# Layer 1's output product for two tiles at once, transposed, in three rounded terms

## The reference

```python
h = layernorm(x) * (1 + scale) + shift
Q, K, V = relu(h @ Wq + bq), relu(h @ Wk + bk), h @ Wv + bv        # 16 heads of 64
# causal linear attention with cos and sin weights of the position (scan over t):
num = qc @ S_cos + qs @ S_sin;  den = max(qc . z_cos + qs . z_sin, 1e-6)
out = (num / den).reshape(B, T, 1024)
x = x + gate * (out @ Wo + bo)                                     # Wo: 1024 x 128
# then a router over 16 experts and the layer's mixture of experts on layernorm(x)
```

## Time and profile before

| what | value |
|---|---|
| median of three runs | 860.9 us (857.6 to 861.99) |
| profiled execution, its span | 860.6 us |
| instructions | 32362 |
| loop of layer 1, PE full | about 310 to 763 us |

### The profile page before, as it was taken

How to read it: one execution, slowest core, us unless ns; L and a number is a source line. 1 busy time by engine, 2 the same in 40 slices (tenths; PEclk the granted TensorE clock), 3 DMA queues, 4 the chain that set the end, 5 groups by cost and what they waited for, 6 DMA issues and landing times.

```text
span 860.6 us, 32362 instructions
## 1 busy us (share of the span) xinstructions
PE 798.8 (93%) x13678; PEld 695.9 (81%) x13678; DVE 611.5 (71%) x1776; ACT 434.6 (50%) x944; POOL 394.6 (46%) x399
## 2 busy tenths in 40 slices
PE   6999984489998799999999999999999999999998
PEld 5777764489997678888889888889888888878887
DVE  7897785357773676676677776787877778757865
ACT  6555533244542665656546566566574645523322
POOL 4357685604544473554645754556643533500000
PEclk9999996599998999999999999999999999999999
DMA  9824000163421200000010000100000000038661
GB/s 294 259 67 161 27 29 13 41 184 102 135 86 45 83 27 4 3 28 4 15 40 4 28 4 3 53 4 4 4 3 3 5 3 3 4 79 148 143 126 39
DMA packets 67904, 49.65 MB, mean 58 GB/s; under 512 B 5322, under 2 KB 62778, under 8 KB 67377
## 3 DMA queue, kind: packets, MB, share of 16 engines
q1 hardware_dynamic: 64288, 42.41, 18.4%
q0 software_dynamic: 3328, 5.16, 1.8%
q10 hardware_dynamic: 144, 0.02, 0.0%
HBM read 33.20 MB, written 16.10 MB: 57 GB/s over the span
## 4 chain that ended last, share of the span: by engine, by line
PE 72%; issue 13%; DVE 6%; DMA 3%; ACT 2%; another core or an unknown queue 1%; SPq 1%; POOL 1%; PEldq 0%; PEld 0%; DVEq 0%; ACTq 0%; POOLq 0%
PE psum L1560 11%; PE psum L1665 7%; PE psum L1716 6%; PE psum L1690 6%; PE psum L1244 6%; PE psum L2349 5%; PE psum L1595 5%; PE psum L1627 5%; PE psum L2367 4%; PE psum L1705 4%; PE psum L1607 3%; PE psum L1578 3%; PE psum L1279 3%; DMA sb_e_x<-disp 1%
## 5 line engine op out<-in xcount | busy, mean ns | idle before, releaser
L1560 PE MATMUL psum<-sb_wkv,sb_a_hs 128*128 128x512 f32 x384 | 122.1, 426 | 1.3 <-ACT sb_a_hs L2036 0.7
L2248 POOL TENSOR_TENSOR sb_a_qr<-sb_h,sb_a_csq 128x512 f32<-128x512 f32 x64 | 81.0, 1288 | 92.0 <-PE psum L1690 88.1
L2248 POOL TENSOR_TENSOR sb_a_qr<-sb_a_qp,sb_a_csq 128x512 f32<-128x512 f32 (+1 forms) x64 | 72.2, 1149 | 94.6 <-PE psum L1690 94.6
L1844 ACT ACTIVATE sb_a_vr<-sb_a_va,sb_consts 128x520 f32<-128x520 f32 x128 | 86.6, 726 | 14.6 <-DVE sb_a_va L2106 14.3
L310 POOL DMA_INDIRECT disp<-sb_h,sb_slot x64 | 67.9, 1062 | 32.2 <-issue 16.9
L1560 PEld LDWEIGHTS psum<-sb_wkv,sb_a_hs 128*128 128x128 f32 x384 | 63.6, 190 | 13.5 <-issue 1.2
L1183 POOL DMA_INDIRECT chosen<-sb_m_h3t,sb_e_row x40 | 39.4, 984 | 69.3 <-ACTq L1357 49.2
L1665 PE MATMUL psum<-sb_a_mid,sb_a_qr 64*64 64x65 f32 x2048 | 70.9, 218 | 0.0
L1244 PE MATMUL psum<-sb_e_xt,sb_e_ws 128*128 128x320 f32 x384 | 65.5, 327 | 5.4 <-issue 4.3
L1690 PE MATMUL psum<-sb_a_vr,sb_a_kb 64*64 64x130 f32 x1920 | 70.1, 272 | 0.0
L1244 PEld LDWEIGHTS psum<-sb_e_xt,sb_e_ws 128*128 128x128 f32 x384 | 59.6, 198 | 9.2 <-issue 5.2
(11 more groups left out here) (289 smaller groups left out, 1986.2 us busy)
## 6 DMA issues: line engine op xcount, KB each, us to landing
sb_h<-turned SPq DMA_DIRECT2D x32, 256.0 KB, 5.5
sb_e_w<-in_w SPq DMA_DIRECT2D x24, 256.0 KB
chosen<-sb_empty SPq DMA_DIRECT2D x8, 512.0 KB, 6.1
sb_a_g<-chosen SPq DMA_DIRECT2D x12, 256.0 KB, 3.1
disp<-sb_empty SPq DMA_DIRECT2D x4, 650.0 KB, 9.9
sb_e_x<-disp SPq DMA_DIRECT2D x7, 325.0 KB
sb_a_wo<-in_wo SPq DMA_DIRECT2D x4, 512.0 KB, 4.5
out<-sb_x SPq DMA_DIRECT2D x7, 256.0 KB, 3.9
```

The source lines that it names most:

```text
L1560: ins = pe.matmul(self.values_bank(i) if kv else self.bank[0], hs[:, part, at:at + P], self.Wkv[ws][:, h, w], start=(k == 0), stop=(k == 2))
L1844: ins = act.activation(self.Vr[i % 2][:, :, k, :], self.Va[i % 3][:], ACT.Copy, scale=self.c[("cos1", "sin1")[k]][:, n:n + 1])
L2248: ins = g.tensor_tensor(self.Qr[i % 2][:, k, :, t], qp, rows(self.csQ[:, k, c * P + t.start:(c + 1) * P], PH), ALU.mult)
```

## The change

- The product is done for two tiles (pair p) at once, at steps i = 4p + 5, and transposed: Wo is stationary, the turned outputs of two tiles are moving, 256 columns wide. Three rounded terms, eight blocks each: 24 matmuls. The exchange of halves is done in the moving operand's reading order.
- ACT's three copies become two: one of bank 3 into a plain buffer oTf (`outputs_scalar`) and, behind it, one that rounds it into oT1[0] (`outputs_high`). POOL makes the rest oT1[1] by a subtraction (`outputs_low`), in every step, behind the queries and ahead of everything else of its step; ACT's next first copy waits for it.
- The gate is no longer in the weights: ACT copies the transposed product to y with the gate's column as scale (`output_gated1`), between its two copies; PE turns y back in the next step (`output_returned`, i = 4p + 6), and DVE adds two tiles to x at once. POOL's four `gate_out` and four loads of Wo go away; Wo is loaded once early (`raw_o`, 512 KB) and split by ACT and DVE at expert 5 of layer 0 (two more pieces; experts 1 to 4 have two each already).
- In the loop the statistics for the router begin at step 3 instead of 2, POOL's roots for it at step 4 instead of 3. `tiles_normed` and `tiles_turned` stay where they are.
- Behind the loop the last pair's product comes after `gate_up_tensor(1, 2)`; the last tiles' statistics, turn and logits, and group 6's router weights (`weights1_parts`) come later.
- To make room some buffers move into others' space, and the DMA scratch of the program is set to 8 KB.

```diff
@@ -1463,7 +1468,7 @@
-        self.Wog = [sb(f"a_wo{k}", [P, HD // P, D]) for k in range(2)]
+        self.Wo = [sb(f"a_wo{k}", [P, HD // P, D], F32R) for k in range(2)]
@@ -1498,9 +1504,8 @@
-        halves = sb("a_ot", [P, HD // P, P])
-        spare = self.h3T[:, (NT - G4) * P:].rearrange("p (m t) -> p m t", t=P)
-        self.oT1 = [[halves[:, 0:PH, :], spare], [halves[:, PH:, :]] * 2]
+        self.oT1 = [sb(f"a_ot{k}", [P, HD // P, 2 * P], F32R) for k in range(2)]
+        self.oTf = sb("a_otf", [P, PH, P])
@@ -1617,7 +1611,8 @@
-        pe.wait_ge(S["c_OTc"], i)
+        if i:
+            pe.wait_ge(S["c_OTc"], 2 * i - 1)
@@ -1631,12 +1626,14 @@
-    OUTPUT_AT = {2 * n + 3: n for n in range(NT - 1)}
+    PAIRS1 = NT // 2
+    OUTPUT_AT = {4 * p + 5: p for p in range(PAIRS1 - 1)}
+    RETURN_AT = {4 * p + 6: p for p in range(PAIRS1 - 1)}
...
-    def output_home(self, n):
-        return self.bank[1][:, 0:D] if n == NT - 1 else self.bank[4][:, 512 - D:512]
+    def output_home(self, p):
+        return self.bank[1] if p == self.PAIRS1 - 1 else self.bank[4]
     def logits_home(self, m):
@@ -1654,7 +1651,9 @@
-            pe.wait_ge(S["c_x"], self.OUTPUT_AT[i] + 1)
+            pe.wait_ge(S["c_y"], self.OUTPUT_AT[i] + 1)
+        if i in self.RETURN_AT:
+            pe.wait_ge(S["c_x"], self.RETURN_AT[i] + 1)
@@ -1707,15 +1706,27 @@
-    def output1_tensor(self, n):
-        pe, S, b = self.pe, self.S, n // TB
-        pe.wait_ge(S["c_OTc"], 2 * n + 2)
-        if n % TB == 0:
-            pe.wait_ge(S["c_Wog"], b + 1)
-        for m in range(HD // P):
-            ins = pe.matmul(self.output_home(n), self.oT1[m // PH][n % 2][:, m % PH, :], self.Wog[b % 2][:, m, :], start=(m == 0),
-                            stop=(m == HD // P - 1))
+    def output1_tensor(self, p):
+        pe, S, out = self.pe, self.S, self.output_home(p)[:, 0:2 * P]
+        pe.wait_ge(S["c_OTl"], 4 * p + 4)
+        for k, (ws, part) in enumerate(((0, 0), (1, 0), (0, 1))):
+            for m in range(HD // P):
+                turned = self.oT1[part][:, m, :].rearrange("p (n r t) -> p n r t", n=2, r=2)
+                if m // 2 % 2:
+                    turned = turned[:, :, ::-1, :]
+                ins = pe.matmul(out.rearrange("p (n r t) -> p n r t", n=2, r=2), self.Wo[ws][:, m, :], turned,
+                                start=(k == 0 and m == 0), stop=(k == 2 and m == HD // P - 1))
...
+    def output_returned(self, p):
+        pe, S, at = self.pe, self.S, 2 * P if p == self.PAIRS1 - 1 else 0
+        pe.wait_ge(S["c_y"], p + 1)
+        for t in range(2):
+            ins = pe.transpose(self.output_home(p)[:, at + t * P:at + (t + 1) * P], self.y[:, t * P:(t + 1) * P],
+                               self.c["ident"])
+        ins.then_inc(S["c_yT"], 1)
     def tiles_turned(self, xn, sem, m, before):
@@ -1774,6 +1785,8 @@
+            if i in self.RETURN_AT:
+                self.output_returned(self.RETURN_AT[i])
@@ -1822,13 +1835,28 @@
     def outputs_scalar(self, i):
-        act, S, h = self.act, self.S, i % 2
+        act, S = self.act, self.S
...
-        act.wait_ge(S["c_Y"], max(0, i // 2 - 1 + h))
-        out, got = self.oT1[h][i // 2 % 2], self.bank[3].rearrange("p (m t) -> p m t", t=P)
-        act.copy(out[:, 0:2, :], got[:, 0:2, :])
-        act.copy(out[:, 2:4, 0:DH], got[:, 2:4, DH:P])
-        act.copy(out[:, 2:4, DH:P], got[:, 2:4, 0:DH]).then_inc(S["c_OTc"], 1)
+        act.wait_ge(S["c_OTl"], i)
+        act.copy(self.oTf[:].rearrange("p m t -> p (m t)"), self.bank[3]).then_inc(S["c_OTc"], 1)
+    def outputs_place(self, part, i):
+        n, h = i // 2, i % 2
+        return self.oT1[part][:, PH * h:PH * (h + 1), n % 2 * P:(n % 2 + 1) * P]
+    def outputs_high(self, i):
+        act, S = self.act, self.S
+        act.wait_ge(S["c_Y"], i // 4)
+        act.wait_ge(S["c_OTc"], 2 * i + 1)
+        act.copy(self.outputs_place(0, i), self.oTf[:]).then_inc(S["c_OTc"], 1)
+    def output_gated1(self, p):
+        act, S, b = self.act, self.S, p // (TB // 2)
+        act.wait_ge(S["c_Y"], p + 1)
+        act.wait_ge(S["c_yT"], p)
+        act.activation(self.y, self.output_home(p)[:, 0:2 * P], ACT.Copy, scale=self.mT[1][:, 2, b:b + 1]
+                       ).then_inc(S["c_y"], 1)
     def keys_cut(self, i):
@@ -1909,6 +1937,10 @@
                 self.hidden_scalar(0, self.HIDDEN[i][0])
             if known(i - 1):
                 self.outputs_scalar(i - 1)
+            if i in self.OUTPUT_AT:
+                self.output_gated1(self.OUTPUT_AT[i])
+            if known(i - 1):
+                self.outputs_high(i - 1)
             if known(i + 1):
                 self.keys_scalar(i + 1)
             if i >= steps - 2:
@@ -2151,12 +2183,13 @@
-    def output1_vector(self, n):
-        v, S = self.dve, self.S
-        x = self.X[:, n, :]
-        v.wait_ge(S["c_Y"], n + 1)
-        v.wait_ge(S["c_xb"], n // G4 + 1)
-        v.tensor_tensor(x, self.output_home(n), x, ALU.add).then_inc(S["c_x"], 1)
+    def output1_vector(self, p):
+        v, S, at = self.dve, self.S, 2 * P if p == self.PAIRS1 - 1 else 0
+        x = self.X[:, 2 * p:2 * p + 2, :]
+        v.wait_ge(S["c_yT"], p + 1)
+        v.wait_ge(S["c_xb"], p // 2 + 1)
+        v.tensor_tensor(x, self.output_home(p)[:, at:at + 2 * P].rearrange("p (n d) -> p n d", n=2), x, ALU.add
+                        ).then_inc(S["c_x"], 1)
     def logits_vector(self, m):
@@ -2192,9 +2225,9 @@
-            if i >= 8 and i % 8 == 2:
+            if i >= 8 and i % 8 == 3:
...
-                parts = self.stats_parts(i // 8 - 1, self.st3, "3", ("c_x", 4 * (i // 8)))
+                parts = self.stats_parts(i // 8 - 1, self.st3, "3", ("c_x", 2 * (i // 8)))
@@ -2206,8 +2239,8 @@
-            if i in self.OUTPUT_AT:
-                self.output1_vector(self.OUTPUT_AT[i])
+            if i in self.RETURN_AT:
+                self.output1_vector(self.RETURN_AT[i])
@@ -2257,11 +2290,12 @@
-    def gate_out(self, b):
+    def outputs_low(self, i):
...
-        g.wait_ge(S[f"dma_wo1_{b % 2}"], 16 * (b // 2 + 1))
-        g.tensor_tensor(self.Wog[b % 2][:], self.Wog[b % 2][:], rows(self.gate[1, 2][:, b, :], HD // P), ALU.mult
-                        ).then_inc(S["c_Wog"], 1)
+        g.wait_ge(S["c_OTc"], 2 * i + 2)
+        g.tensor_tensor(self.outputs_place(1, i), self.oTf[:], self.outputs_place(0, i).bitcast(F32), ALU.subtract
+                        ).then_inc(S["c_OTl"], 1)
     def l1_gpsimd(self):
@@ -2278,21 +2312,22 @@
         for i in range(steps):
             if known(i + 1):
                 self.queries_gpsimd(i + 1)
+            if known(i - 1):
+                self.outputs_low(i - 1)
             if known(i) and i % 8 == 0 and i // 8 + 2 < NGRP:
                 self.mix(g, i // 8 + 2)
             if i == 1:
                 self.bias_added(1)
-            if i % 8 == 3 and i >= 8:
+            if i % 8 == 4 and i >= 8:
                 self.roots(i // 8 - 1, self.rt3, "3")
             if i % 8 == 5 and i // 8 + 2 < NGRP:
                 self.roots(i // 8 + 2, self.rt1, "1")
             if i % 8 == 7 and i // 8 + 2 < NGRP:
                 self.low_part(g, i // 8 + 2)
                 self.bias_added(i // 8 + 2)
-            if i in (25, 41):
-                self.gate_out((i + 7) // 16)
             if i in (52, 60):
                 self.down_gated((i - 52) // 8)
+        self.outputs_low(steps - 1)
         self.roots(NGRP - 1, self.rt3, "3")
         for b in range(2, B):
             self.down_gated(b)
@@ -2394,19 +2429,21 @@
         self.hidden_product(1, 0, 0)
         self.outputs_turned(steps - 1)
         self.hidden_product(1, 0, 1)
-        self.output1_tensor(NT - 1)
-        pe.wait_ge(S["c_OTc"], steps)
         self.gate_up_tensor(1, 1)
         pe.wait_ge(S["c_On"], steps)
         self.gate_up_tensor(1, 2)
+        self.output1_tensor(self.PAIRS1 - 1)
         self.gate_up_tensor(1, 3)
+        self.output_returned(self.PAIRS1 - 1)
+        pe.wait_ge(S["c_OTc"], 2 * steps - 1)
         self.down_tensor(0)
-        self.tiles_turned(self.xn1, "c_xn3", NGRP - 1, [("c_x", NT), ("c_lg", NGRP - 1)])
         self.gate_up_tensor(1, 4)
         for gi in range(2, NGRP):
             for j in range(MB + 1):
                 self.gate_up_tensor(gi, j)
                 if (gi, j) == (2, 0):
+                    self.tiles_turned(self.xn1, "c_xn3", NGRP - 1, [("c_x", self.PAIRS1), ("c_lg", NGRP - 1)])
+                if (gi, j) == (2, 2):
                     self.logits_tensor(NGRP - 1, [])
                 if j == 1:
                     self.down_tensor(gi - 1)
@@ -2442,17 +2479,20 @@
         steps = 2 * NT
         self.hidden_scalar(1, 0)
         self.outputs_scalar(steps - 1)
+        self.outputs_high(steps - 1)
         self.hidden_scalar(1, 1)
         self.hidden_scalar(1, 2)
+        self.output_gated1(self.PAIRS1 - 1)
         self.hidden_scalar(1, 3)
         self.split_scalar(2)
```

(22 more changed lines are left out.)

30 lines of the change are left out of this document (13 added, 17 removed).

## The result

The changed kernel takes 894.2 us (median; 892.9 to 896.5) where the kernel before, on the same chip, takes 861.3: a ratio of 1.040, 95% interval 1.036 to 1.043. Slower, as forecast, but by 33 us where 5 were forecast, and outside the range.

The account below looks back on a forecast made before the run. PE, busy 93% of the span, was taken as the bound. On 860.6 us the terms -9.7 - 1.8 + 11.2 + 1.8 + 1.8 + 1.7 = +5.0 gave 865.6, forecast as 866; eight in ten from 854 to 874.

Parts of the forecast that it names:

- The first paragraph: Layer 1's loop: PE is full, 57.52 us in eight steps, so a microsecond taken from PE is a microsecond of time.
- PE's gain, -9.7: Output product in the loop: fifteen new pairs at 3.05 us replace 31 old products at 1.79 us, 9.7 us gained.
- The wait for the roots, +11.2: Router's turn: PE waits 1.6 us for POOL's roots, now behind its subtraction, seven times, 11.2 us.
- DVE and the ports, +1.8 and +1.8: Loop: DVE late in short steps, 1.8 us; POOL's subtraction against DVE at shared ports, 0 to 3.6, taken as 1.8.
- the first +1.8: DVE in three successive short steps: the next starts about 0.45 us late, 0.3 reaching PE, six times, 1.8 us.
- The lock's rule: POOL and DVE share an exclusive port lock, held for the whole instruction; all four waits would come, 1.8 us more.
- The tail, -1.8: Behind the loop, sixteenth pair: 3.2 us gained at the down product less a 1.4 us wait, 1.8 us gained.
- The first half: Behind the loop: down product starts 1.3 us earlier, straight behind other work, and the half clock goes, 3.2 us gained.
- the wait that I put at 1.4 us: Behind the loop: group 6's router operations on DVE move ahead of a weighting the next down product needs, 1.4 us.
- The clock in the loop, +1.7: Loop: new 1.6 us waits may halve the clock, 1.7 us each, 0 to 11.9; one drop taken, 1.7 us.
- At nothing: Costed at zero: ACT's extra 0.55 us a step, the gate's copy, POOL's removed work, the early load, the 8 KB scratch.

Follow-up runs that it names:

- e6: Changed kernel padded with 247 tiny products in 16 steps, counted to keep instruction-block borders out of most uncovered dense stretches: 890.6 us, ratio 1.033.
- e7: Changed kernel without POOL's subtraction; the third term reads the high part again, so PE's instructions stay the same: 888.0 us, ratio 1.030.
- e9: Changed kernel with the 247 tiny padding products and POOL's roots put ahead of its subtraction: 890.1 us, ratio 1.031.
- e14: Changed kernel with the 247 tiny padding products and without POOL's subtraction: 873.6 us, ratio 1.016.
- e2: Changed kernel with 64 tiny products (256 PE instructions, a whole block) added once, in step 4: 903.5 us, ratio 1.046.
- e3: Changed kernel with 370 tiny products in 16 steps, placed by a wrong instruction count: 930.0 us, ratio 1.080.
- e10: Changed kernel with 183 tiny products placed anew in 17 steps and POOL's roots ahead of its subtraction: 887.9 us, ratio 1.026.
- e8: Kernel before with one more ACT copy of 512 elements a row in each step, result unread: 861.1 us, ratio 0.999.
- e11: Kernel before with only the change's 8 KB DMA scratch: 863.9 us, ratio 1.001.
- e5: Kernel before with 32 tiny products (128 PE instructions, half a block) to four corners, once in step 4: 904.5 us, ratio 1.051.
- e1: Kernel before with 64 tiny products (256 PE instructions) to one corner of the array, once in step 4: 871.0 us, ratio 1.008.

## Why the prediction was wrong

The direction was right; the size was not, because the largest term, +32.4 us, was not in the sum. The direction was in part luck: the forecast's own terms as measured, -7.8 + 2.0 + 5.2 + 3.1 = +2.5, are next to nothing, and the +11.2 that carried it showed with 2.0.

- **The first paragraph is the step that failed.** From "PE works all 57.52 us" it took that a microsecond taken from PE is one of time. But PE was full because its program arrived in time, and a change of what PE's program contains moves every border behind it. The sum has no term for that. The sign stood in the earlier trace rows: 1.20 us of "issue" between 30 and 2 products of one group. I used that row for the clock alone and didn't ask what could stop an engine that waits for nobody. The dense stretches last 37.4 us longer than 64 x 2.98 in the changed kernel and 5.0 in the one before: the 32.4 us.
- **PE's gain, -9.7**: measured -7.8. 24 products take 2.95 us and not 2.83, the spacing being 0.123 and not 0.118; two turns back 0.22, as said. The blocked, exchanged operand costs 5 ns a matmul at most.
- **The wait for the roots, +11.2**: the chain was right in each link and 1.67 us long (e6), but in the changed kernel it shows in 3 of 7 places, 2.0 us, and the longest, 1.46 us in the last group, is there without the subtraction too (e7). It was covered by the pauses: two costs in one place don't add. It was also not only an order on POOL: with the roots first 1.07 of 1.67 us stay (e9). Taking the subtraction away from the padded kernel brings what the prediction gave it, and more: 16.9 us (e14), where 11.2 + 1.8 stood.
- **DVE and the ports, +1.8 and +1.8**: measured +5.2 ahead of the outputs' turn, 1.4 us in each of three steps and 0.7 in a fourth. All of it goes with the subtraction (e7), so three short steps in a row, the first +1.8, cost nothing by themselves. For the ports I had said 0 to 3.6, by waits of 0.9 us; two operations one after the other are held up in such a step. The lock's rule was right and I took half of it. The chain of waits of the changed kernel:

```profile
475.26 1.25 DVE sb_rows L2605
476.51 0.02 issue
476.54 1.21 DVE sb_m_comb L2610
```

- **The tail, -1.8**: measured +3.1. The first half went as forecast: the first down product follows other work without a wait and takes 4.70 us at the full clock. But ahead of the second the wait that I put at 1.4 us is 3.1, for DVE does 3.0 us of router operations between two weightings (from 810.47), and the half clock comes there, for longer. The busy times of the stretch, columns as above:

```profile
813.10:819.90 6.80, 5.62 (x26) 5.62 (x27) 4.71 (x12) 1.92 (x4) 0.00 (x0) 0.52 0.69 143
```

and the down product in the chain of waits:

```profile
814.28 7.51 PE psum L2402 x40
```

6.8 us at 0.52 where the earlier trace rows had 3.4, and this second down product takes 7.51 us, where it took 4.62. Part of it is this execution's own: in seven of the eight other variants of the changed kernel the half clock lasts 3.4 us there, in e6 there is none, and the part from the last scores on takes 99.0 to 101.0 us in them (102.2 here), 97.1 to 99.7 in the variants of the kernel before (99.0).
- **The clock in the loop, +1.7**: nothing in the changed kernel. Pauses of 0.3 to 2.0 us come 24 times, and the granted clock stays at 1.00 from 297 to 792 us. The risk was real all the same: in seven of its variants (e2, e3, e6, e7, e9, e10, e14) PE's clock is at half for 3.4 us once to three times in the loop, ten times in all.
- **At nothing**: ACT's copies (e8) and the scratch (e11), rightly.
- In the loop, -7.8 + 32.4 + 5.2 + 2.0 = 31.8 of 33.7 us. 1.2 of the other 1.9 are one wait at 349.0 us ahead of the turned keys, for ACT (line 1895), which the kernel before does not have; e7 and e14 have it too, so it is not the subtraction's. The rest I can't place.

## What to carry to other kernels

An engine that is full with small instructions lives on its program's arriving in time; "issue" in the midst of a group of one line is the sign. Number the engine's instructions and look at the remainder of 256 before taking such pauses for waits. Then a time can't be compared across a change of the instruction count without asking where the borders lie: add half a block and a whole block of cheap work to both kernels and compare the best of each. And keep a coarse piece of work ahead of a dense stretch; the old product, in every second step, did that unasked.

## What the runs showed of the hardware

- PE's instructions come in blocks of 256 (16.4 KB), one transfer of 0.9 to 1.4 us each, and PE goes on 1.2 to 1.6 us behind its end, 77 times in four traces. Dense 64x64 products use one up in 2.35 us. What starts a transfer I couldn't settle: many begin about 1 us behind the border before (the median in the changed kernel's loop is 1.0), some 3 to 5 us behind it, then 0.2 to 1.1 us behind a wait in PE's queue, mostly one ahead of the products with the state.
- 32 products of 64x64 that go to four corners of the array take 1.1 us (17 ns a record, e5); 64 of them to one corner take 7.6 us, 0.12 each (59 ns a record, e1).
- Pauses of up to 2.04 us didn't lower the granted clock in any of the changed kernel's 24 cases. In seven of its variants ten stretches of 3.4 us at the lower of the two levels begin 0.1 to 1.4 us behind the end of idle time of 1.6 to 2.2 us, ended by DVE, by ACT's tiles or by "issue" (e2 at 464.6, behind 2.07 us of "issue"). Idle time of the same length was followed by it in some cases and not in others.
